# A Mamba-2 block with an fp8-style feed-forward: where the decay exponents are computed, and how the feed-forward's row blocks follow each other

## The reference, cut to what matters

```python
x = x + mamba(layernorm(x)); x = x + ffn(layernorm(x))
# mamba: 128 heads of 64, 8 groups of B and C (state 128), chunks of 128 tokens, two per batch
gate, hBC, dt = split(x @ in_proj_w.T);  hBC = silu(conv4(hBC) + conv_b)
dt = clip(softplus(dt + dt_bias), 0, 100);  A_cum = cumsum(dt * -exp(A_log)) # in each chunk
Y_diag = (C B^T * L) @ (hs * dt),  L[l, s] = exp(A_cum[l] - A_cum[s]) for s <= l
Y_off  = what the first chunk's state adds to the second, decayed likewise
y = (Y + hs * D) * silu(gate);  RMS norm over each group of 1024 columns, * norm_w;  @ out_proj_w.T
# ffn: every 128-column block of an activation is divided by (max|x| / 448 + 1e-12) and multiplied back
h = silu(q(x) @ W1.T) * (q(x) @ W3.T);  y = q(h) @ W2.T      # 512 -> 1792 -> 512, W = wq * scale per 128x128 block
```

## Time and profile before

| | us |
|---|---|
| median of 3 runs | 1919.47 (1918.16 to 1920.56) |
| the profiled execution | 1918.38 |
| its span, first to last instruction | 1916.6 |
| TensorE busy | 1820.9 |
| POOL busy | 1006.9 |
| VectorE busy | 1301.1 |
| ScalarE busy | 918.7 |

### The profile page before, as it was taken

How to read it: one execution, slowest core, us unless ns; L and a number is a source line. 1 busy time by engine, 2 the same in 40 slices (tenths; PEclk the granted TensorE clock), 3 DMA queues, 4 the chain that set the end, 5 groups by cost and what they waited for, 6 DMA issues and landing times.

```text
span 1916.6 us, 37316 instructions
## 1 busy us (share of the span) xinstructions
PE 1820.9 (95%) x11192; PEld 1484.7 (77%) x11192; DVE 1301.1 (68%) x2149; ACT 918.7 (48%) x1660; POOL 1006.9 (53%) x802
## 2 busy tenths in 40 slices
PE   5799999999999999999999999999999977989898
PEld 4677787778777877787778777877887756878887
DVE  6588638863886388638863886388648857777776
ACT  3566536643664366436643664366436632212221
POOL 4266636663666366536653666366636665233220
PEclk9899999999999999999999999999999988999999
DMA  2211101110111011101110111011101110111101
GB/s 91 61 52 51 34 12 51 51 33 12 51 51 33 12 51 51 33 12 51 51 33 12 51 51 33 12 51 51 33 12 52 40 48 20 41 44 36 40 11 45
DMA packets 43639, 74.90 MB, mean 39 GB/s; under 512 B 10356, under 2 KB 11508, under 8 KB 43608
## 3 DMA queue, kind: packets, MB, share of 16 engines
q1 hardware_dynamic: 42600, 73.12, 12.1%
q10 hardware_dynamic: 1008, 1.38, 0.2%
HBM read 70.35 MB, written 4.06 MB: 39 GB/s over the span
## 4 chain that ended last, share of the span: by engine, by line
PE 87%; DVE 8%; issue 2%; POOL 1%; ACT 1%; DVEq 0%; POOLq 0%; ACTq 0%
PE proj L743 15%; PE proj L745 15%; PE proj L744 15%; PE y L875 6%; PE y L929 6%; PE y L931 5%; PE y L930 5%; PE y L865 3%; PE trb L842 3%; PE diff L851 3%; DVE gated L1234 2%; PE misc L851 1%; PE y L743 1%; PE y L744 1%; PE y L745 1%
## 5 line engine op out<-in xcount | busy, mean ns | idle before, releaser
L743 PE MATMUL proj<-xhi,w_hi 128*128 128x512 f32 x1088 | 465.9, 428 | 5.6 <-DVE v L1057 5.6
L745 PE MATMUL proj<-xhi,w_lo 128*128 128x512 f32 x1088 | 425.9, 391 | 0.0
L744 PE MATMUL proj<-xlo,w_hi 128*128 128x512 f32 x1088 | 425.6, 391 | 0.0
L392 POOL TENSOR_TENSOR w_lo<-w_raw,w_hi 128x512 fp32r<-128x512 f32 x144 | 184.2, 1298 | 227.9 <-ACT w_hi L522 227.9
L1057 DVE SCALAR_TENSOR_TENSOR v<-proj,par_sb,v 128x510 f32<-128x510 f32 (+2 forms) x384 | 281.9, 741 | 15.0 <-ACT v L544 11.7
L448 POOL TENSOR_TENSOR g_lo<-gated,g_hi 128x512 fp32r<-128x512 f32 x128 | 164.8, 1290 | 190.4 <-ACT g_hi L675 189.8
L743 PEld LDWEIGHTS proj<-xhi,w_hi 128*128 128x128 f32 x1088 | 205.0, 188 | 75.2 <-issue 7.9
L745 PEld LDWEIGHTS proj<-xhi,w_lo 128*128 128x128 f32 x1088 | 204.8, 188 | 46.4
L744 PEld LDWEIGHTS proj<-xlo,w_hi 128*128 128x128 f32 x1088 | 205.4, 189 | 38.6
L1152 DVE TENSOR_TENSOR M<-diff,cb 128x512 f32<-128x512 f32 x256 | 170.1, 686 | 81.4 <-ACT diff L630 81.4
L929 PE MATMUL y<-wo_hi,g_hi 128*128 128x512 f32 x512 | 204.3, 399 | 5.5 <-POOL g_lo L448 5.1
(11 more groups left out here) (179 smaller groups left out, 3718.1 us busy)
## 6 DMA issues: line engine op xcount, KB each, us to landing
w_raw<-in_win SPq DMA_DIRECT2D x144, 256.0 KB, 2.7
wo_raw<-in_wout SPq DMA_DIRECT2D x64, 256.0 KB, 2.6
M<-in_w SPq DMA_DIRECT2D x14, 512.0 KB, 3.3
cb<-in_w SPq DMA_DIRECT2D x7, 512.0 KB, 3.3
row_l<-rows_l SPq DMA_DIRECT2D x192, 6.0 KB
out<-resid SPq DMA_DIRECT2D x8, 256.0 KB, 2.0
rows_l<-gated SPq DMA_DIRECT2D x9, 128.0 KB, 2.5
resid<-in_x SPq DMA_DIRECT2D x4, 256.0 KB, 4.6
```

Of the source, the lines that this page charges most:

```text
L392: e.tensor_tensor(w_lo[:, slot, i, :], w_raw[:, i, :], w_hi[:, slot, i, :].bitcast(F32), ALU.subtract).then_inc(split.sem, 1)
L743: e.matmul(o, hi_l, hi_r, start=first, stop=False)
L744: e.matmul(o, hi_l, lo_r, start=False, stop=False)
L745: return e.matmul(o, lo_l, hi_r, start=False, stop=last)
```

## The change

**Decays.** The running sums stay fp32. They are stored once to DRAM (`sums`), and per head one row of 1024 is loaded to all 128 partitions (`load_row`, 512 KB in SBUF). What is subtracted or added per partition stands in a small table `offsets` (24 columns a tile), loaded per tile. ScalarE makes the exponent as it reads the row, with the offset as bias. The own-chunk decays of a head fill two banks (`own`, 1024 columns), the cross ones `misc`; TensorE's exponent matmuls and the bf16 parts go. Head 0 of the next tile is done in the step before (`ahead`), for a new group in the window. SP's loads and ScalarE's order move with it.

```diff
+            def decay_own(g, j, par_, head):
+                act.wait_ge(s_row[head], (16 * TPG * (2 - head)) * g + (32 - 16 * head) * j + 16)
+                act.wait_ge(mdone.sem, mdone.at(g, j, 2 * head - 1))
+                for z in range(2):
+                    for b in range(B):
+                        block = 2 * b + z
+                        at = head * NB + block
+                        ins = e.activation(diff[z][:, b * P:(b + 1) * P], row[:, head, block * P:(block + 1) * P],
+                                           ACT.Relu, scale=-1.0, bias=offset[:, par_, at:at + 1])
+                ins.then_inc(dbound.sem, 1)
+                act.wait_ge(dbound.sem, dbound.at(g, j, head + 1))
+                e.activation(own[:, :], own[:, :], ACT.Exp, scale=-1.0).then_inc(edone.sem, 1)
+            def decay_past(g, j, par_, head):
+                for b in range(B):
...
+                    ins = e.activation(misc[:, b * P:(b + 1) * P], row[:, head, block * P:(block + 1) * P],
+                                       ACT.Exp, bias=offset[:, par_, at:at + 1])
 # ScalarE's step: own(j, 1), past(j, 1), tap3(0), upper_pair, tap3(1), hs_tanh(0), own(j+1, 0), hs_tanh(1),
 # past(j+1, 0), gate_tanh(0), scale and round wo, gate_tanh(1)
 # VectorE's step: times_dt(0), weigh_own(j, 1), times_dt(1), weigh_past(j, 1), conv_rest(0), conv_rest(1) with
 # hs_silu(0) in it, weigh_own(j+1, 0), hs_silu(1), gate_silu(0), weigh_past(j+1, 0), y sums, gate_silu(1)
 # TensorE's step: turn(0), unit(0), turn(1), unit(1), y() of 48 matmuls, unit(2), unit(3)
             def step(g, j, par_, nxt, nxt2, ahead):          # SP
                 sp.wait_ge(wolo.sem, wolo.at(g, j, 0))
                 sp.dma_start(wo_raw[:, :], wout[TPG * g + j, :, :]).then_inc(woraw.sem, 16)
                 if nxt:
-                    sp.wait_ge(dready.sem, dready.at(g, j, 1))
-                    load_rows(TPG * g + j + 1, 1 - par_)
+                    sp.wait_ge(edone.sem, edone.at(g, j, 2))
+                    load_offset(TPG * g + j + 1, 1 - par_)
+                    load_row(TPG * g + j + 1, 0)
                 if nxt2:
                     load_pair(9 * g + j + 3, split.at(g, j, 0))
+                if nxt:
+                    sp.wait_ge(edone.sem, edone.at(g, j, 4))
+                    load_row(TPG * g + j + 1, 1)
+                    if i == 12 and nxt:                      # ScalarE's window, behind g_upper(12)
+                        act.wait_ge(cbd.sem, cbd.at(g + 1, 0, 0))
+                        decay_own(g + 1, 0, 0, 0)
+                        decay_past(g + 1, 0, 0, 0)
```

```diff
-                for w in range(2):
-                    for k in range(KD):
-                        mm = three(proj[t % 2][:, w * FC:(w + 1) * FC],
...
+                for k in range(KD):
+                    mm = three(proj[t % 2][:, :],
+                               xhi[:, k, t * P:(t + 1) * P], xlo[:, k, t * P:(t + 1) * P],
+                               up_hi[par_][:, k, :], up_lo[par_][:, k, :], k == 0, k == KD - 1)
+            def requantise(dst, src, t, blocks):
+                for n in range(blocks):
+                    cols = slice(n * QB, (n + 1) * QB)
+                    ins = e.tensor_scalar(dst[:, cols], src[:, cols], qr[:, t % 2, n:n + 1], qs[:, t % 2, n:n + 1],
+                                          ALU.mult, ALU.mult)
 # VectorE's hidden():
-                g2, h = fh[:, t % 2, :], fh[:, 2 + t % 2, :]
+                g2, h = fh[:, t % 2, :], proj[t % 2][:, FC:2 * FC]
                 chain(e.scalar_tensor_tensor(g2, g2, 1.0, proj[t % 2][:, 0:FC], ALU.add, ALU.mult))
+                chain(e.scalar_tensor_tensor(h, g2, 0.5, h, ALU.mult, ALU.mult))
+                reciprocals(t, h, proj[t % 2][:, 0:2], 2, chain)
                 dve.wait_ge(f_tr, n + 1)
...
+                requantise(fh[:, 2 + t % 2, :], h, t, 2).then_inc(f_h, 1)
 # VectorE's chunk(): hidden of the next row block now comes ahead of h_lower(t)
```

More of the change, by code:

```diff
@@ L288, in _ @@
[L288 to L296, removed]
@@ new lines, in load_row, with load_offset @@
+            def load_row(t, head):
+                sp.dma_start(row[:, head, :],
+                             sums[bass.ds(2 * t + head, 1), :].rearrange("a f -> (a f)").partition_broadcast(P))\
+                    .then_inc(s_row[head], 16)
+            def load_offset(t, par_):
+                sp.dma_start(offset[:, par_, :], offsets[:, bass.ds(t, 1), :].rearrange("p a k -> p (a k)"))\
+                    .then_inc(s_row[0], 16)
+            for h in range(2):
+                sp.wait_ge(s_cumread, h + 1)
+                sp.dma_start(halves(sums, h), halves(acum, h)).then_inc(s_rows, 16)
@@ L305, in step @@
+            sp.wait_ge(s_rows, 32)
+            load_row(0, 0)
+            load_row(0, 1)
+            sp.wait_ge(s_off, 6)
+            sp.dma_start(offsets.rearrange("p t k -> p (t k)"), offset_all).then_inc(s_rows, 16)
+            sp.wait_ge(s_rows, 48)
+            def step(g, j, par_, nxt, nxt2, ahead):
                 sp.wait_ge(wolo.sem, wolo.at(g, j, 0))
@@ L731, in chunk @@
                         weights_upper(c + 1, 1 - par_, t // 2)
+                    if first and t in (1, 2):
+                        x_upper(n2, TT - 3 + t)
                     h_upper(t)
@@ L959, in _ @@
[L959 to L970 removed]
+                pe.wait_ge(f_h, TT * c + t + 1)
@@ new lines, in gate_up, with down @@
+                if first:
+                    pe.wait_ge(n2["lower"], t + 1)
+                for k in range(KD):
+                    mm = three(proj[t % 2][:, :],
+                               xhi[:, k, t * P:(t + 1) * P], xlo[:, k, t * P:(t + 1) * P],
+                               up_hi[par_][:, k, :], up_lo[par_][:, k, :], k == 0, k == KD - 1)
+                mm.then_inc(f_gu, 1)
+            gate_up(0, 0, 0, True)
+            def down(c, par_, t):
+                pe.wait_ge(f_lod, 3 * c + 3)
+                pe.wait_ge(f_htl, TT * c + t + 3)
+                pe.wait_ge(f_acc, TT * c + t + 1)
+                for k in range(2):
+                    mm = three(ybank[t % 2][:, :], ht_hi[:, t % 2, k, :], ht_lo[:, t % 2, k, :],
+                               down_hi[par_][:, k, :], down_lo[par_][:, k, :],
+                               k == 0, k == 1)
+                mm.then_inc(f_y, 1)
@@ L980, in chunk @@
                     pe.wait_ge(f_htl, TT * c + t + 1)
+                    if first and t < 4:
+                        pe.wait_ge(n2["lower"], t + 5)
                     for k in range(2):
@@ L983, in chunk @@
                     mm.then_inc(f_tr, 1)
-                down(TT - 1)
+                if not nxt:
+                    down(c, par_, TT - 1)
             over_chunks(pe, chunk)
```

579 lines of the change are left out of this document (265 added, 314 removed).

## The result

The changed kernel took 1926.25 us (median of 6 runs, 1923.05 to 1931.25), the kernel before 1917.83 us on the same chip (6 runs, 1915.2 to 1920.56): ratio 1.0044 [1.0029, 1.0060]. It is slower by 8 us where I had put 1845, and lies outside my range of 1776 to 1904. Its profiled execution has a span of 1924.4 us.

The account below looks back on a forecast made before the run. TensorE bound the kernel before; after, a 16.3 us ScalarE-VectorE ring was to set the step. From 1918.4 us: steps -24, windows +12, last window and feed-forward -53, start -10, giving 1843.6, forecast 1845; range 1776 to 1904.

Parts of the forecast that it names:

- the second ring: Steps: POOL's wo_lo, SP's loads of wo_raw, offsets, row and w_raw, then ScalarE; 16.0 us, just hidden.
- the case: Steps: slow row broadcasts delay w_raw on SP's queue; 1903 us at 2.6 us a row; chance 0.20.
- lands over 4 us after its issue: Steps: a row landing this late was named as a sign that the forecast is wrong.
- The first ring: Steps: weighing decays, VectorE's convolution, ScalarE's tanh and both heads' exponents; 16.3 us, setting the step.
- Rival (c): Steps: narrow activations don't overlap, 0.41 us each; group 143 us, 1975 in all; chance 0.10 including anything down to 0.34.
- Rival (a): Steps: TensorE stays the bound, bias free, narrow activations 0.20 us; steps 15.0 us, 1780 in all; chance 0.16.
- near 95% busy: Sign for the forecast in the steps: ScalarE's busy share between 84 and 1500 us.
- Windows: Head 0's decays amid the roundings of g stall TensorE 1.75 us before block 13; seven windows, +12 us.
- Last window and feed-forward: End of kernel: earlier turn of x, gate_up starting at once, row blocks of 4.4 us; -53 us.
- the stretched multiply: Feed-forward before: one row block in two waits for a 0.43 us multiply stretched to 1.86 us.
- Start: Before the first unit: three-part splitting with its stores and loads goes; first unit near 74 us; -10 us.
- The sum for a group: Steps of one group: 127.7 us against 130.7 to its last matmul; eight groups, -24 us.

Follow-up runs that it names:

- experiment 1: Changed kernel with the two w_raw loads issued ahead of the offsets and head 0's row on SP: 1858.85 us, ratio 0.9697.
- experiment 2: Changed kernel with row loads cut from 128 partitions to 16 in the steps (decays of the others wrong): 1843.35 us, one run.
- experiment 6: Changed kernel with w_raw loaded ahead of offsets and row, and wo scaled and rounded before the first tanh: 1816.33 us, ratio 0.9475.
- experiment 7: On top of experiment 6, head 0's decays of the next group behind the window's 16th rounding of g, not the 13th: 1815.69 us, ratio 0.9469.
- experiment 5: Changed kernel with only the scaling and rounding of wo moved ahead of the first tanh, row still before w_raw: 1817.24 us, one run.

## Why the prediction was wrong

**The step that failed** is the second ring: "the broadcast takes 1.3 us if it reads like them [...] second w_raw landed after 5.9 us [...] 16.0 us. It is just hidden." The row took 5.0 us from issue to landing, the pieces of w_raw behind it 4.8 instead of 2.7, and the second piece was in 7.8 us after the end of wo_lo, where my sum had 5.9: ScalarE's second rounding, which starts with it, begins at 352.54 (353.16, the end of the pair, less 0.62), and wo_lo ended at 344.78. The other two terms held: 1.29 us of wo_lo for 1.3, and 8.9 of ScalarE up to the next wo_lo (361.45) for 8.8. The ring is 17.95 us long, not 16.0, and sets the step. It missed in rate, not in structure. From 346 on, the queue moved

```profile
346.00:347.00 1.00, 1.00 (x7) 0.88 (x7) 0.00 (x0) 0.97 (x2) 1.00 (x2) 1.00 0.98 235
347.00:348.00 1.00, 1.00 (x6) 0.81 (x5) 0.84 (x1) 1.00 (x5) 1.00 (x2) 1.00 0.73 114
348.00:349.00 1.00, 1.00 (x6) 0.69 (x4) 1.00 (x3) 0.97 (x2) 0.92 (x2) 1.00 1.09 274
...
351.00:352.00 1.00, 1.00 (x23) 1.00 (x20) 0.85 (x2) 0.14 (x1) 1.00 (x1) 1.00 1.07 424
```

(last two columns: DMA share and GB/s) 114 to 274 GB/s at a busy share of 0.73 to 1.09 up to 351, and 424 only at the end. My 400 GB/s came from large packets of a stretch with one kind of load. I had named the case, bounded it and priced it (the row "lands over 4 us after its issue" as the sign, slower than before from 2.9 us), and given it 0.20; by its scale (1903 at a step of 17.4, 64 steps) the average step of 17.8 us is 1929, of which 4.6 us came back in the feed-forward and 1.3 at the start: 1923 for 1926. The mistake was to take the fast end of an unmeasured rate when the slack behind it was 0.3 us: the chance should have gone the other way.

A page of the Trainium skill, "DMA: Bandwidth & Descriptors" (Where 436 GB/s comes from), puts the memory side at about 358 GB/s for each of the two cores that share it. The trace does not show that limit (424 in one microsecond), and by an estimate from the page 512 KB at 358 would have taken 1.5 us, so the rule would not have warned either.

**The first ring**: right. 16.4 (experiment 1, in the steps that the row does not hold up) and 16.34 us (experiment 2) for 16.3. Eight narrow activations with a bias take 2.41 us, thus 0.293 from start to start ((2.41 - 0.356) / 7), where I had 0.30; the wide Exp 1.01 for 1.0. Rival (c) falls. The Trainium skill's "ScalarE: Activation LUTs" (What ACT_TABLE_LOAD costs) gives 0.294, and the trace agrees. Each is 0.356 long, not 0.38. ScalarE "near 95% busy" was a wrong sign: 997.7 of 1468 us after, and 1046.6 of 1461 in experiment 1, where this ring does bind, since the windows lie in the stretch and leave it idle.

**Rival (a)**, TensorE's floor of 15.0: about right, and not the bound. The first step of a group, whose head 0 is done in the window, runs on TensorE without a wait; in the kernel after, from its first turn to the next:

```profile
274.93 0.60 PE L865 MATMUL trb<-ident,hs 128*128 128x128 f32 x4
...
289.72 0.60 PE L865 MATMUL trb<-ident,hs 128*128 128x128 f32 x4
```

That is 14.79 us (14.79 to 14.83 in every group but the first), where I had 14.8. The 15.74 us of experiment 6 are 0.95 more. Inside a unit the matmuls stay 0.23 us apart there; the excess stands where units and turns meet (0.24 for 0.03 us ahead of unit 0, 0.48 for 0.23 ahead of turn(1), 0.39 for 0.23 ahead of unit 3). The busy share of 98% hides such short waits, since the ends of matmuls are modelled. What ends them is open.

**Windows**: +1.8 for 1.75 us each. The waits of a window stand ahead of its blocks for g_lo, the longest where I had put it, against the earlier trace rows:

```profile
466.88 0.50 PE L929 MATMUL y<-wo_hi,g_hi 128*128 128x512 f32 x1 [1.66 <-POOL g_lo L442]
```

But experiment 7 shows that the term was no separate one: without the stall the first step gives the time back.

**Last window and feed-forward**: -57.6 for -53; row block 4.33 for 4.4 us. From the last sums of squares to the first transposes of h it is 59.8 us, in place of 82.6; I had 60.4. The reason was half right. I had seen the stretched multiply go, and the wide matmuls are 7.6 us of it as computed. But not one row block in two waits for such a multiply: 17 of 55 do, and the average of 5.03 us before (I had 4.9) has the chunks' ends in it. That a tiny operation would be caught by the new order, and that keeping two maxima in PSUM spares it 18.6 us, I had not seen, though the first line of the earlier trace rows is such an operation (1.26 us for 128x8, 0.17 in the median of its group). The diff did both at once, so the sum held by luck in this term.

**Start**: -11.3 for -10.

**The sum for a group** has a slip: 8 x 16.3 - 2.1 - 0.4 is 127.9, not 127.7. That is 1.6 us over the kernel and changes nothing.

## What to carry to other kernels

When a load moves into a queue ahead of another one, follow the ring through that queue and ask how much slack it has; if that is less than the uncertainty of the load's duration, put the load behind the others, or move the work that releases the queue (here one move of two activations, 109 us). Price a broadcast from memory as its full volume at the rate of a mixed queue, not at the best rate seen. In VectorE's dependent chains beside a busy POOL, keep even the smallest operands in PSUM; if they stay in SBUF, the order decides whether they begin early or late in POOL's operation, and so what they wait.

## What the runs showed of the hardware

- A row of 4 KB broadcast to 128 partitions (512 KB) lands 5.0 us after its issue in the changed kernel, 128 different rows 4.5, 64 KB 2.4; loads of 256 KB behind it go from 2.7 to 4.8 us. The 5.0 us is no fixed price: with the loads spread differently over the step the same row landed in 3.9 (experiment 5) and 3.7 us (experiment 6).
- A VectorE TENSOR_SCALAR of 128x2 from SBUF to SBUF takes 0.17 us alone. When it begins beside a POOL TENSOR_TENSOR of 128x1024, it ends with that: 2.02 to 2.05 us with 2.0 us of POOL's operation to go, 0.50 with 0.48 to go (the kernel before), 0.17 with 0.1 to go. With its source in PSUM it takes 0.16 beside the same operation. RECIPROCAL of the same size on SBUF and SCALAR_TENSOR_TENSOR with one operand in PSUM showed no stretch here. The Trainium skill's "SBUF — State Buffer" (SBUF: two separate sides) says that VectorE in a two-port mode or with two SBUF inputs shares an exclusive pair of ports with GpSimd, held for a whole instruction; "VectorE: DVE Perf Modes" (Why PSUM operands drop a tier) that an operand in PSUM rules the two-port mode out. The trace agrees on both counts, down to two columns.
